# An audio tower kernel: input loaded first, row scales of the first pair spread by TensorE, and new positions for the steps of all stages

## The chip, the cores and the metric

One core of one Trainium2 chip. The metric is device time in microseconds (us) of one execution, the median of several runs; less is better. Beside it stands one profiled execution, whose trace gives every instruction its start, its duration and what released it.

## The reference

```python
# x: 16 batches x 128 channels x 750 steps, f32
fwd = ewma_scan(xt); bwd = ewma_scan(xt[::-1])[::-1]         # carry = 0.1*x + 0.9*carry
h = einsum('btc,dc->btd', (fwd + bwd) * 0.5, W) + b           # D = 256
hidden = layernorm(h)                                          # no gain, no shift
for l in range(2):                                             # N = 64 states
    delta = softplus(hidden @ Wd[l] + bd[l]); u = hidden @ Wi[l] + bi[l]
    decay = exp(-delta * softplus(A_log[l])); drive = delta * u
    hs = scan over t of (s = decay*s + drive)
    hidden = hs @ Wo[l] + bo[l] + (final @ Ws[l] + bs[l])      # class row
h = h + hidden
xf = layernorm(h)
shared = (silu(xf @ shared_gate.T) * (xf @ shared_up.T)) @ shared_down.T   # 512 wide
scores = sigmoid(xf @ router_w.T); sb = scores + correction_bias
# 16 experts in 4 groups; the 2 best groups by the sum of their 2 best, then the 4 best experts
w = scores of the 4 / their sum
routed = sum over the 4 of (w * silu(xf @ gate[e]) * (xf @ up[e])) @ down[e]  # 64 wide each
out = h + shared + routed                                      # 12,000 tokens x 256
```

## The kernel before

The 16 batches are worked in 8 pairs of 1500 tokens. A pair's tokens are cut into three stretches of 500, and those into 12 tiles of 125 tokens. The work falls into three kinds.

- **The chain** turns a pair's input into tokens with their LayerNorm and their place in the experts' lists. Its steps are `ewma`, `ewma_back` (the two scans, VectorE), `tok` (the token product, TensorE, evacuated to `h` and measured by VectorE), `ln1_stats` (variance by VectorE, the power -0.5 by GpSimd, L716), `pre(layer, s)` (both projections of one layer for one stretch), `ssm_log`, `ssm_decay`, `ssm_scan` (softplus, decay, scan), `split`, `carry` and `class_row` (parts of the next layer's input), `y(s, half)` (output product of the last layer, added to `h` by VectorE at L1147), `residual` (GpSimd adds the class row to `h`, L725), `ln2_stats`, `ln2_norm`, `x2t` (transposes), `logit`, the `route_*` and `place_*` steps (top experts and each token's place), `entries` (L1311, the positions), `list` 0 to 11 (GpSimd scatters a tile's entries into the lists in DRAM, L732), and `table` (L1379 to L1382, the first row of each list, needed by the next pair).
- **Shared slots** (S): 12 in a pair, one for each quarter of the shared network's hidden units and stretch of 500 tokens (L1605, L1392).
- **Expert blocks** (B): 99 in all, each 128 entries of one of six lists (one for each pair of groups). GpSimd gathers the rows (L753), TensorE transposes them (`bx`, L1650), multiplies by the weights of two groups (L1630) and transposes the hidden units back (`bh`, L1658), ACT and VectorE scale and split them (L1401, L1406, L1416, L1422), TensorE multiplies by the down weights (L1689), and GpSimd adds the rows to the output in DRAM (`add_to_out`, L764). A B slot of pair q works on entries that earlier pairs put into the lists.

Time is counted in ticks, 24 for each pair. `SHARED` and `ROUTED` (L17, L18) say which ticks hold which kind of slot. The table `CHAIN` (L21) says for each step where it stands on each engine, in ticks from the beginning of the pair's own slots (negative: while the pair before has the slots); `EARLY` (L121) holds exceptions for single pairs, and `PREPARE` (L134) the positions of the weights' preparation. From these `ticks` builds one fixed order of instructions for each engine. Nothing is reordered at run time: an instruction that waits holds up all that stand behind it on its engine. The tables fix only the order; how long a tick lasts comes out of the work.

On TensorE all chain products and the transposes `bx` and `bh` share two PSUM banks, `ch_ps`, used in turn. `bank_is_free` makes each user wait until the user two turns before has been evacuated:

```python
if g is not None and slot(g - 2)[0] == "B":
    in_turn.append(("bh", 0, slot(g - 2)[1]))
if g is not None and slot(g + 2)[0] == "B":
    in_turn.append(("bx", 0, slot(g + 2)[1]))
```

In the first pair nothing is there yet to fill TensorE. SP issues the token weight `tok_w` (L565), then the input of both batches (L567); ACT issues the token bias as the first of its queue. VectorE and TensorE together prepare the token weight (`tokw` 0, L960 and L962 on VectorE), and VectorE then scans. The row scales `rstd` (one number for each token, tokens in the partitions) are needed along the free axis for `pre(0, s)`. Their way is: transpose on TensorE (L1526), ACT to `rstd_rows` (L821), SP stores them to DRAM (L626), and SP loads them back three times, spread to all partitions (L635), into `rb[s]`; VectorE multiplies by them at L1104.

## Time and profile before

| | before |
|---|---|
| three runs, us | 1368.88, 1370.2, 1370.58 (median 1370.2) |
| profiled execution, us | 1365.87 |
| its span (first to last instruction), us | 1364.1 |
| granted TensorE clock, mean | 0.928 of full |
| TensorE busy | 1181.2 us, 87% |
| VectorE busy | 923.1 us, 68% |
| GpSimd busy | 582.2 us, 43% |
| ACT busy | 542.1 us, 40% |
| DMA | 71.04 MB, mean 52 GB/s |

A granted clock of 1.00 is TensorE at 2.4 GHz, 0.50 at 1.2 GHz; a stretch between them spent a part at each. In rows of the trace PE is TensorE, DVE VectorE, POOL GpSimd, SPq and ACTq the sequencers of SP and ACT when they issue DMAs. A row of a timeline gives start, duration, engine, line and operation, and in brackets how long the engine had stood idle before it and what released it.

### The profile page before, as it was taken

How to read it: one execution, taken by the hardware profiler on the slowest of the kernel's cores; microseconds unless marked ns; L12 is line 12 of the kernel's file. 1: busy time of each engine (PE TensorE's matmuls, PEld its weight loads, DVE VectorE, ACT ScalarE, POOL GpSimd, SP SyncE). 2: the span in 40 equal slices, each digit the busy share in tenths (PEclk: the TensorE clock that was granted, in tenths of full speed). 3: DMA queues.
4: the chain of work that ended last, by engine and by line, in shares of the span. 5: the costliest groups of instructions: out<-in, count | busy, mean ns of one | idle time of the engine just before them, and what ended most of it. 6: DMA issues, size and time to landing. Idle time of an engine off the chain costs nothing.

```text
span 1364.1 us, 24631 instructions
## 1 busy us (share of the span) xinstructions
PE 1181.2 (87%) x7454; PEld 1067.0 (78%) x7454; DVE 923.1 (68%) x2326; ACT 542.1 (40%) x893; POOL 582.2 (43%) x428
## 2 busy tenths in 40 slices
PE   3459858987999699987999699987999889998997
PEld 3348647777988688876888689876988788898997
DVE  6786996977578765876578764877578644654443
ACT  1424613542355235532355134442355233223332
POOL 2053272084515643284514634176423632375543
PEclk9558987998999899998999799998999989999999
DMA  3503112121411123121411223121221213223321
GB/s 73 121 27 96 31 29 81 32 52 28 115 32 41 38 55 75 32 49 48 88 41 33 41 55 82 32 46 49 47 74 37 42 47 58 42 51 57 56 34 17
DMA packets 84543, 71.04 MB, mean 52 GB/s; under 512 B 36302, under 2 KB 79119, under 8 KB 84424
## 3 DMA queue, kind: packets, MB, share of 16 engines
q0 software_dynamic: 22272, 25.51, 11.7%
q1 hardware_dynamic: 59920, 43.55, 11.2%
q8 instruction: 72, 1.18, 0.4%
q10 hardware_dynamic: 2232, 0.42, 0.2%
q14 instruction: 47, 0.39, 0.1%
HBM read 32.13 MB, written 38.60 MB: 52 GB/s over the span
## 4 chain that ended last, share of the span: by engine, by line
PE 56%; DVE 15%; issue 11%; POOL 10%; ACT 3%; DMA 3%; SPq 1%; POOLq 0%; DVEq 0%; ACTq 0%
PE gu_ps L1630 15%; PE gu_ps L1605 12%; PE d_ps L1689 10%; PE d_ps L1671 5%; POOL lists L732 4%; PE ch_ps L1582 3%; PE ch_ps L1658 2%; PE ch_ps L1521 2%; POOL block_rows L753 2%; POOL h L725 2%; PE ch_ps L1531 1%; POOL out_dram L764 1%; DMA x_in<-in_x_dram 1%; DVE fw L1049 1%; PE ch_ps L1650 1%
## 5 line engine op out<-in xcount | busy, mean ns | idle before, releaser
L889 ACT ACTIVATE hid<-gu_ps 128x512 f32<-128x512 f32 (+1 forms) x195 | 115.1, 593 | 366.3 <-PE gu_ps L1630 262.1
L764 POOL DMA_INDIRECT out_dram<-block_rows,entry x99 | 157.4, 1590 | 226.2 <-ACT block_rows L901 203.2
L1630 PE MATMUL gu_ps<-gu_hi,bx_hi 128*128 x792 | 243.5, 307 | 10.0 <-issue 10.0
L1630 PE MATMUL gu_ps<-gu_hi,bx_lo 128*128 x792 | 229.5, 290 | 0.0
L1630 PE MATMUL gu_ps<-gu_lo,bx_hi 128*128 x792 | 229.2, 289 | 0.0
L732 POOL DMA_INDIRECT lists<-listed,pos x96 | 126.6, 1319 | 185.5 <-DVE pos L1311 160.0
L1671 PE MATMUL d_ps<-down,hid 128*125 128x256 f32 x768 | 188.1, 390 | 0.0
L1630 PEld LDWEIGHTS gu_ps<-gu_hi,bx_hi 128*128 128x128 f32 x792 | 157.1, 198 | 18.3 <-issue 16.9
L1671 PEld LDWEIGHTS d_ps<-down,hid 128*125 128x125 f32 x768 | 142.9, 194 | 20.0 <-issue 0.3
L1630 PEld LDWEIGHTS gu_ps<-gu_hi,bx_lo 128*128 128x128 f32 x792 | 157.3, 199 | 1.2
L1630 PEld LDWEIGHTS gu_ps<-gu_lo,bx_hi 128*128 128x128 f32 x792 | 155.7, 197 | 0.0
L753 POOL DMA_INDIRECT block_rows<-token_rows,entry x99 | 116.5, 1177 | 49.2 <-issue 25.0
L1422 DVE TENSOR_TENSOR hid_lo<-ch_ps,hid_hi 128x512 fp32r<-128x512 f32 x99 | 67.9, 686 | 97.0 <-ACT hid_hi L906 97.0
L1689 PE MATMUL d_ps<-dr_hi,hid_hi 128*128 x396 | 117.9, 298 | 7.8 <-DVE h L1412 7.8
L1689 PE MATMUL d_ps<-dr_hi,hid_lo 128*128 x396 | 112.4, 284 | 0.0
L1689 PE MATMUL d_ps<-dr_lo,hid_hi 128*128 x396 | 112.3, 284 | 0.0
L720 POOL TENSOR_TENSOR rstd<-mv,mhalf 125x4 f32<-125x4 f32 x24 | 27.8, 1157 | 197.4 <-DVE mv L1090 197.3
L1401 DVE TENSOR_TENSOR gu_ps<-gu_ps,entry 128x512 f32<-128x512 f32 x99 | 69.7, 704 | 26.6 <-PE gu_ps L1630 22.6
L1157 DVE TENSOR_TENSOR x_lo<-ch_ps,x_hi 128x500 fp32r<-128x500 f32 x48 | 32.0, 677 | 80.0 <-ACT x_hi L873 80.0
L901 ACT ACTIVATE block_rows<-d_ps 128x256 f32<-128x256 f32 x99 | 38.0, 383 | 121.1 <-PE d_ps L1689 121.1
L1689 PEld LDWEIGHTS d_ps<-dr_hi,hid_hi 128*128 128x128 f32 x396 | 75.7, 191 | 12.3 <-issue 11.5
L725 POOL TENSOR_TENSOR h<-h,rows 125x512 f32<-125x512 f32 x48 | 65.2, 1378 | 43.3 <-DVE rows L1139 42.9
(271 smaller groups left out, 2981.4 us busy)
## 6 DMA issues: line engine op xcount, KB each, us to landing
token_rows<-xn SPq DMA_DIRECT2D x24, 500.0 KB
out_dram<-h SPq DMA_DIRECT2D x24, 500.0 KB
t<-rstd_scratch SPq DMA_DIRECT2D x24, 250.0 KB, 5.1
x_in<-in_x_dram SPq DMA_DIRECT2D x15, 375.0 KB, 3.5
entry<-lists SPq DMA_DIRECT2D x99, 8.0 KB, 3.0
block_rows<-token_rows,entry POOLq DMA_INDIRECT x99, 2.9
out_dram<-block_rows,entry POOLq DMA_INDIRECT x99, 3.8
lists<-listed,pos POOLq DMA_INDIRECT x96, 2.6
```

Of the source, the lines that this page charges most:

```text
L725: inc(pool.tensor_tensor(hv, hv, row, ALU.add), "res_done")
L732: pool.indirect_dma_start(out=lists, out_offset=bass.IndirectOffsetOnAxis(pos[:, arg:arg + 1], 0), in_=listed[:, arg, :], in_offset=None). ...
L753: pool.indirect_dma_start(out=block_rows[u], out_offset=None, in_=token_rows[0:there, :], in_offset=bass.IndirectOffsetOnAxis(entry[n % UE ...
L764: pool.indirect_dma_start(out=out_rows[0:there, :], out_offset=bass.IndirectOffsetOnAxis(entry[n % UE][:, ID:ID + 1].bitcast(U32), 0), in_ ...
L889: inc(act.activation(hid[g % 4][:, 0:n], gu_ps[:, 2 * (g % 2), 0:n], ACT.Silu), "silu_done")
L1401: inc(dve.tensor_tensor(up, up, w, ALU.mult), "up_weighed")
L1422: inc(dve.tensor_tensor(hid_lo[g % 2][:], ch("bh", 0, n), hid_hi[g % 2][:].bitcast(F32), ALU.subtract), "b_lo")
L1582: last = pe.matmul(bank[0:TP, j * 64:j * 64 + e1], xx[:, k, j * TP:(j + 1) * TP], rw[:, k, 0:e1], start=(n == 0), stop=(n == len(parts) - ...
L1605: last = pe.matmul(bank, w[:, k, ms], xx[:, k, :], start=(k == 0 and q == 0), stop=(k == KD - 1 and q == 2))
L1630: last = pe.matmul(gu_ps[:, 2 * (g % 2) + half, q * GH:(q + 1) * GH], a[n % 2][:, k, :], w[:, k, bass.ds(of, 1), half * GH:(half + 1) * GH ...
L1671: last = pe.matmul(d_ps[0:TP, j, :], hid[g % 4][:, tc], down[:, m, :], start=(m == 0 and j % 2 == 0), stop=(m == M - 1), skip_group_check= ...
L1689: last = pe.matmul(d_ps[:, 2 * (n % 2), :], a[g % 2][:, m * P:(m + 1) * P], rows_[:, bass.ds(of, 1), half * D:(half + 1) * D].rearrange("p ...
```

## The change

- The input is loaded first. `tok_w` goes to ACT's queue, ahead of the bias, which has a signal of its own (`w_tokb`). `tokw` 0 moves from -34.6 to -32.2, that is behind the first batch's forward scan on VectorE.
- The first pair's row scales are spread by TensorE: for each stretch of 500 a new step `rstd_row` multiplies the column of scales, broadcast to 128 columns, by the identity, four times 125 columns, and ACT copies the bank to `rb[s]`. The store and the three loads of the first pair go away; the other pairs keep them.
- With the spread gone from SP for the first pair, SP's `loads` (weights of the shared network and the experts) directly follow the load of the third batch (L617).
- The preload of the exponential's table on ACT goes away for the first pair's second layer (L839).
- `SHARED` and `ROUTED`: the slots at ticks 12 and 13 to 16 change places, so that the B slot of tick 12 is now at tick 16. Many positions in `CHAIN`, `EARLY` and `PREPARE` are new. What they change in the order of each engine, where the work is that the trace shows waiting: on VectorE `entries` come ahead of one evacuation of the second layer (L1114) and two products of a B slot (L1406), and behind one of an S slot (L1392); `table` 1 and `table` 3 come earlier; `y(0,0)` comes behind a product of a B slot; a pair of additions (L1412) comes ahead of `y(0,1)`, where it had stood ahead of `y(1,1)`; and `ln2_norm` 0 (L1093) comes ahead of `y(1,1)`. On GpSimd `list` 9 comes behind the next batch's forward and backward sum (L709), `list` 11 ahead of `residual` 3, and in the first pair ten lists stand ahead of the residual, not nine. On ACT `score_exp` comes half a tick earlier.

```diff
-SHARED = (0, 1, 2, 3, 7, 8, 9, 10, 13, 14, 15, 16)
-ROUTED = (4, 5, 6, 11, 12, 17, 18, 19, 20, 21, 22, 23)
+SHARED = (0, 1, 2, 3, 7, 8, 9, 10, 12, 13, 14, 15)
+ROUTED = (4, 5, 6, 11, 16, 17, 18, 19, 20, 21, 22, 23)
...
-    ("ewma", 0, dict(SP=-32.0, DVE=-33.5, POOL=-29.0, ACT=-28.5)),
+    ("ewma", 0, dict(SP=-33.5, DVE=-33.5, POOL=-29.0, ACT=-28.5)),
-    ("ewma", 1, dict(SP=-23.5, DVE=-28.5, POOL=-27.0, ACT=-26.5)),
+    ("ewma", 1, dict(SP=-25.5, DVE=-28.5, POOL=-27.0, ACT=-26.5)),
-    ("spread", 0, dict(SP=-22.0)),
+    ("spread", 0, dict(SP=-23.5)),
+    ("rstd_row", 0, dict(PE=-22.0, ACT=-21.5)),
+    ("rstd_row", 1, dict(PE=-22.0, ACT=-21.5)),
+    ("rstd_row", 2, dict(PE=-22.0, ACT=-21.5)),
-    ("ssm_log", 1, dict(ACT=-10.0, DVE=-11.0)),
+    ("ssm_log", 1, dict(ACT=-10.0, DVE=-10.5)),
-    ("y", (0, 0), dict(PE=-5.5, DVE=-6.0)),
+    ("y", (0, 0), dict(PE=-5.5, DVE=-5.5)),
-    ("ln2_stats", 0, dict(DVE=-4.5, POOL=-4.5)),
+    ("ln2_stats", 0, dict(DVE=-4.5, POOL=-4.0)),
-    ("ln2_norm", 0, dict(DVE=-3.5, ACT=-3.5)),
+    ("ln2_norm", 0, dict(DVE=-4.0, ACT=-3.5)),
-    ("ln2_stats", 1, dict(DVE=-3.0, POOL=-4.0)),
+    ("ln2_stats", 1, dict(DVE=-2.5, POOL=-2.0)),
-    ("score_exp", 0, dict(ACT=5.5)),
-    ("route_pairs", 0, dict(DVE=7.5)),
+    ("route_pairs", 0, dict(DVE=6.0)),
+    ("score_exp", 0, dict(ACT=5.0)),
-    ("list", 9, dict(POOL=18.5)),
+    ("list", 9, dict(POOL=19.5)),
-    ("table", 1, dict(DVE=16.5)),
+    ("table", 1, dict(DVE=16.0)),
-    ("table", 3, dict(DVE=17.5)),
-    ("list", 11, dict(POOL=20.0)),
+    ("table", 3, dict(DVE=17.0)),
+    ("list", 11, dict(POOL=19.5)),
...
 PREPARE = (
-    (-34.6, "tokw", 0),
+    (-32.2, "tokw", 0),
-    (-21.5, "loads", 0),
+    (-22.0, "loads", 0),
-    (-14.9, "fold", 3),
+    (-16.9, "fold", 3),
-    (3.4, "routed", 1),
+    (2.9, "routed", 1),
...
 # SP
-            sp.dma_start(wraw, tok_w.rearrange("(k p) c -> p k c", p=P)).then_inc(S["w_tok"], 16)
...
 # ACT
-            act.dma_start(tokb_bc[:], tok_b.partition_broadcast(TP)).then_inc(S["w_tok"], 16)
+            act.dma_start(wraw, tok_w.rearrange("(k p) c -> p k c", p=P)).then_inc(S["w_tok"], 16)
+            act.dma_start(tokb_bc[:], tok_b.partition_broadcast(TP)).then_inc(S["w_tokb"], 16)
...
+                elif step == "rstd_row":
+                    wait(act, "ew_lo_done", 2)
+                    wait(act, "rstd_row_mm", arg + 1)
+                    inc(act.activation(rb[arg], ch(step, arg, pair)[:, 0:TT], ACT.Copy), "rb_ev")
...
                 elif step == "ssm_log":
-                    act.preload_act_table(ACT.Exp)
+                    if pair or arg == 0:
+                        act.preload_act_table(ACT.Exp)
...
 # VectorE, pre(0, s)
-                        wait(dve, f"rb{s}", 16 * (pair + 1))
+                        if pair == 0:
+                            wait(dve, "rb_ev", s + 1)
+                        else:
+                            wait(dve, f"rb{s}", 16 * pair)
...
 # TensorE
+                elif step == "rstd_row":
+                    wait(pe, "rstd1", 1)
+                    for j in range(SUB):
+                        last = pe.matmul(bank[:, j * TP:(j + 1) * TP],
+                                         rstd[0][:, arg * SUB + j:arg * SUB + j + 1].broadcast_to([TP, P]),
+                                         ident[0:TP, 0:TP], start=True, stop=True)
+                    inc(last, "rstd_row_mm")
```

## Rows read from the trace of the kernel before

**Rows 1.** The chain that ended last, shares of the span by engine, from the page.

```profile
PE 56%; DVE 15%; issue 11%; POOL 10%; ACT 3%; DMA 3%; SPq 1%; POOLq 0%; DVEq 0%; ACTq 0%
```

**Rows 2.** Windows: stretch, length, busy us of each engine, granted clock, DMA share, GB/s.

```profile
0.00:107.00 107.00, 51.16 (x208) 43.24 (x209) 82.32 (x197) 33.29 (x43) 25.44 (x27) 0.67 0.32 76
...
550.00:700.00 150.00, 133.16 (x843) 120.18 (x842) 103.44 (x257) 61.45 (x102) 67.25 (x49) 0.94 0.23 51
...
1225.00:1364.10 139.10, 126.72 (x1055) 126.09 (x1053) 57.35 (x98) 46.53 (x100) 67.50 (x51) 0.97 0.27 41
```

**Rows 3.** TensorE's waits, 107 to 1200 us: total us, times, longest.

```profile
PE ch_ps L1573 <- DVE hid_lo L1422: 24.1, 4, 6.2
PE ch_ps L1573 <- DVE h L1147: 23.2, 7, 6.6
```

**Rows 4.** Timeline of VectorE in the fourth pair's slots, 607 to 625 us.

```profile
607.01 0.69 DVE L1147 TENSOR_TENSOR h<-ch_ps,h 125x512 f32<-125x512 f32 x1 [5.47 <-POOL h L725]
612.02 1.93 DVE L1082 TENSOR_TENSOR mv<-stats 125x4 f32<-125x4 f32 x1
...
617.43 1.94 DVE L1043 TENSOR_SCALAR ends<-x_in 128x2 f32<-128x2 f32 x1 [1.38 <-DMA x_in<-in_x_dram]
...
624.42 1.28 DVE L1412 TENSOR_TENSOR h<-d_ps,h 125x512 f32<-125x512 f32 x2
```

**Rows 5.** Timeline of GpSimd in the same slots, 598 to 620 us.

```profile
597.99 1.61 POOL L764 DMA_INDIRECT out_dram<-block_rows,entry  x1 [0.30 <-issue]
605.63 3.73 POOL L725 TENSOR_TENSOR h<-h,rows 125x512 f32<-125x512 f32 x3
610.89 1.21 POOL L732 DMA_INDIRECT lists<-listed,pos  x1 [0.30 <-issue]
619.27 1.05 POOL L720 TENSOR_TENSOR rstd<-mv,mhalf 125x4 f32<-125x4 f32 x1
```

**Rows 6.** The first transfer of input: its issue and landing; then its kind's median, from the page.

```profile
L567 SPq DMA_DIRECT2D x_in<-in_x_dram x1: 457/457/457, 1.3 to 1.3; - x1
DMA to landing us min/median/max: 7.1/7.1/7.1
x_in<-in_x_dram SPq DMA_DIRECT2D x15, 375.0 KB, 3.5
```

**Rows 7.** Timelines of the start: VectorE, ACT, TensorE.

```profile
8.15 0.42 DVE L962 SCALAR_TENSOR_TENSOR tw_lo<-gu_ps,tw_hi 128x256 fp32r<-128x256 f32 x1
25.95 0.20 ACT L802 ACTIVATE spt<-vecs 128x2 f32<-128x2 f32 x1 [5.83 <-DMA corr_bc<-ffn_correction_bias_dram]
32.42 0.37 PE L1526 MATMUL ch_ps<-ident,rstd 125*12 125x125 f32 x1 [6.28 <-POOL rstd L716]
32.55 0.76 PE L1543 MATMUL ch_ps<-ew_hi,f_hi 128*128 128x500 f32 x1
38.07 0.73 DVE L1104 SCALAR_TENSOR_TENSOR zt<-ch_ps,cb,t 64x500 f32<-64x500 f32 x1 [8.19 <-DMA t<-rstd_scratch]
41.06 1.06 PE L1484 MATMUL gu_ps<-ident,h 128*128 128x128 f32 x4
66.31 0.94 DVE L1118 TENSOR_TENSOR t<-t 128x750 f32<-128x750 f32 x1 [0.95 <-ACT t L851]
89.62 0.67 DVE L1147 TENSOR_TENSOR h<-ch_ps,h 125x512 f32<-125x512 f32 x1
90.99 0.15 DVE L1093 SCALAR_TENSOR_TENSOR nmr<-mv,rstd 125x4 f32<-125x4 f32 x1
```

**Rows 8.** Timeline of VectorE in the first pair's slots, at 185 us.

```profile
184.75 4.36 DVE L1382 TENSOR_SCALAR table<-route_t 1x6 int32<-1x6 f32 x1
```

**Rows 9.** Timeline of VectorE ahead of the fourth pair's positions.

```profile
574.93 0.60 DVE L1114 TENSOR_SCALAR t<-zt,bias1s 128x750 f32<-128x750 f32 x1
575.45 0.68 DVE L1406 TENSOR_TENSOR hid<-hid,gu_ps 128x512 f32<-128x512 f32 x1
```

**Rows 10.** TensorE's only wait of note in the tail, 1225 to 1364 us.

```profile
PE ch_ps L1650 <- DMA block_rows<-token_rows,entry: 3.5, 1, 3.5
```

More of the change, by code:

```diff
@@ L57 @@
     ("split", (1, 1), dict(ACT=-6.0, DVE=-7.0)),
-    ("residual", 5, dict(POOL=-2.0)),
-    ("y", (0, 0), dict(PE=-5.5, DVE=-6.0)),
+    ("residual", 5, dict(POOL=-1.5)),
+    ("y", (0, 0), dict(PE=-5.5, DVE=-5.5)),
     ("y", (0, 1), dict(PE=-5.0, DVE=-4.5)),
-    ("ln2_stats", 0, dict(DVE=-4.5, POOL=-4.5)),
+    ("ln2_stats", 0, dict(DVE=-4.5, POOL=-4.0)),
     ("y", (1, 0), dict(PE=-4.5, DVE=-4.5)),
-    ("ln2_norm", 0, dict(DVE=-3.5, ACT=-3.5)),
+    ("ln2_norm", 0, dict(DVE=-4.0, ACT=-3.5)),
     ("y", (1, 1), dict(PE=-4.0, DVE=-4.0)),
@@ L101 @@
     ("place_sum", 0, dict(DVE=10.0)),
+    ("route_marks", 2, dict(DVE=12.5)),
     ("list", 1, dict(POOL=13.0)),
     ("list", 2, dict(POOL=14.0)),
-    ("list", 3, dict(POOL=14.0)),
+    ("list", 3, dict(POOL=14.5)),
     ("list", 4, dict(POOL=15.5)),
@@ L123 @@
     (1, "table", 3): dict(DVE=19.5),
-    (1, "list", 11): dict(POOL=22.0),
+    (1, "list", 11): dict(POOL=21.5),
     (1, "list", 6): dict(POOL=16.5),
@@ L129 @@
     (1, "list", 8): dict(POOL=19.5),
-    (1, "table", 0): dict(DVE=14.0),
+    (1, "table", 0): dict(DVE=14.5),
+    (0, "list", 0): dict(POOL=11.0),
+    (0, "ln1_stats", 0): dict(POOL=-22.0),
+    (0, "list", 8): dict(POOL=12.5),
+    (1, "ln2_norm", 1): dict(ACT=-1.5),
+    (1, "x2t", (0, 0)): dict(ACT=-3.5),
+    (1, "x2t", (0, 1)): dict(ACT=-3.5),
+    (0, "residual", 4): dict(POOL=-1.5),
+    (0, "residual", 5): dict(POOL=-1.5),
+    (0, "ln2_stats", 0): dict(POOL=-3.5),
+    (0, "ln2_stats", 1): dict(POOL=-3.0),
+    (0, "ln2_stats", 2): dict(POOL=-1.0),
+    (0, "list", 7): dict(POOL=17.0),
+    (0, "list", 6): dict(POOL=17.0),
+    (0, "list", 9): dict(POOL=17.5),
+    (0, "list", 10): dict(POOL=17.5),
+    (1, "y", (2, 1)): dict(PE=-1.5, DVE=-1.5),
+    (1, "table", 1): dict(DVE=16.0),
+    (1, "table", 2): dict(DVE=17.0),
+    (1, "route_weights", 0): dict(DVE=13.0),
+    (0, "list", 3): dict(POOL=16.0),
+    (0, "list", 4): dict(POOL=17.0),
+    (0, "list", 5): dict(POOL=19.0),
+    (1, "list", 10): dict(POOL=20.5),
+    (0, "ewma_back", 1): dict(DVE=-28.0),
+    (1, "place_hot", 0): dict(DVE=8.5),
+    (0, "list", 11): dict(POOL=19.0),
+    (1, "list", 1): dict(POOL=11.5),
+    (1, "list", 2): dict(POOL=12.5),
+    (1, "list", 3): dict(POOL=13.0),
+    (1, "list", 4): dict(POOL=14.0),
+    (1, "list", 5): dict(POOL=16.0),
+    (1, "rstd_row", 0): dict(ACT=-15.5),
 }
 PREPARE = (
-    (-34.6, "tokw", 0),
+    (-32.2, "tokw", 0),
     (-28.0, "tokw", 1),
@@ L247, in ticks @@
             for step, arg, at in CHAIN:
+                if q and step == "rstd_row" or q == 0 and step in ("rstd_t", "spread"):
+                    continue
                 if engine in at:
@@ L461, in audio_tower_kernel @@
         NAGGR = 7
-        PE_STEPS = ("tok", "rstd_t", "pre", "carry", "class_row", "y", "x2t", "logit", "place")
+        PE_STEPS = ("tok", "rstd_row", "rstd_t", "pre", "carry", "class_row", "y", "x2t", "logit", "place")
         in_turn = []
@@ L486, in bank_is_free @@
             elif was == "rstd_t":
-                wait(pe, "rstd_ev", pair + 1)
+                wait(pe, "rstd_ev", pair)
+            elif was == "rstd_row":
+                wait(pe, "rb_ev", arg + 1)
             elif was == "pre":
@@ L624, in chain @@
                 elif step == "spread":
-                    wait(sp, "rstd_ev", pair + 1)
+                    wait(sp, "rstd_ev", pair)
                     sp.dma_start(rstd_dram[pair].rearrange("t (j p) -> (t j) p", p=TP),
@@ L630, in chain @@
                     wait(sp, "st_lo", 4 * pair)
-                    if pair == 0:
-                        wait(sp, "ew_lo_done", 2)
-                    wait(sp, "rstd_st", 16 * (pair + 1))
+                    wait(sp, "rstd_st", 16 * pair)
                     for s in range(NT):
@@ L714, in chain @@
                     wait(pool, "aggr1", NAGGR * (pair + 1))
-                    wait(pool, "rstd_mm", pair)
+                    if pair == 1:
+                        wait(pool, "rstd_row_mm", NT)
+                    else:
+                        wait(pool, "rstd_mm", pair - 1)
                     inc(pool.tensor_tensor(rstd[0][:], mv[0][:, :, 1], mhalf[:], ALU.pow), "rstd1")
```

46 lines of the change are left out of this document (23 added, 23 removed).

## Prediction

> **What bounds the kernel now.** First the page's chain of work that ended last [rows 1]: more than half is TensorE, then VectorE, then GpSimd. No engine bounds the kernel alone, so a stretch is read by what TensorE waits for. Second, the windows [rows 2]: in the first 107 us TensorE is busy for 51, and the start is bound by VectorE and by waits; in the middle it is busy 133 of 150 us at a granted clock of 0.94; in the tail 127 of 139 at 0.97. A microsecond taken from the middle is worth it only where TensorE stands still for it. Third, TensorE's own waits [rows 3]: two stand out, both at the products of `y` (L1573), both for a bank to be evacuated by VectorE. The one behind `hid_lo` comes four times for 6.0 us each, once in each set of slots of the third to sixth pair; the one behind `h` (L1147) seven times, 23.2 us in all.
>
> Fourth, the timelines of VectorE and GpSimd in one such set [rows 4, 5]. VectorE stood idle for 5.47 us until GpSimd had added the class row to `h`, and began `y(0,0)` at 607.01. GpSimd had begun these additions at 605.63, behind lists, gathers and scatters that follow each other 0.30 apart. VectorE then works without a break to 625, but for 1.38 us for the input, so what stands in that row delays `hid_lo` and TensorE's second stall. So the cause of both stalls is how late GpSimd's row of transfers ends, and this begins when VectorE gives the positions (`entries`). I read the change by that chain.
>
> **The change part by part** (+ is time gained).
>
> *Input first.* The input was issued at 1.3 and took 7.1 us, twice the 3.5 us of later loads [rows 6]. It is issued 0.5 us earlier and with `tok_w` no longer ahead of it; I take a landing near 7.6 in place of 8.4. The forward scan begins that much sooner, but the two operations of `tokw` 0 (L962 has 0.42 us, its partner the same [rows 7]) now stand behind it and not in the wait for the input. 0.8 less 0.84: 0. Bounds: -0.9 if the landing doesn't move, +2.5 if it falls to 3.5 us and the token weight is then what is waited for.
> That both loads of batch 0 and 1 and the weights slow each other is what rows 6 suggest. The Trainium skill (DMA: Bandwidth & Descriptors, Issuing engines are not separate DMA queues) says that DMAs of all issuing engines run on the same 16 engines and interleave, so that another issuer saves issue time alone. By that the term is the 0.5 us of issue less 0.84, that is -0.3; the trace agrees so far.
>
> *The weights' loads.* With the spread gone, SP issues megabytes of them behind the third batch's input, 16 us sooner, beside ACT's twelve small loads, for whose last bytes ACT already waits 5.83 us (L802 at 25.95 [rows 7]). They can be as much slower as the input was at 7.1 against 3.5: -3.6. I take -1.5, as VectorE takes the result up later; the other end is 0.
>
> *Row scales.* Before: TensorE's transpose at 32.42, VectorE goes on at 38.07 after 8.19 us idle [rows 7]. After: three times four products. Four of 128x128 took 1.06 us at half clock (L1484), so the three end at 35.6, and ACT's copies (0.7 each by VectorE's 0.67 for 512 columns) lie beside them but for the last, which `pre(0,0)` doesn't need for its bank. Its three products of 500 columns (first 0.76) take 1.6: 37.2, thus +0.9. Bounds: each copy in series, 32.4 + 3 x 1.76 + 1.6 = 39.3: -1.2; the products at twice the speed and 1.3 less for `pre`: +3.
>
> *Table load dropped.* VectorE waited 0.95 us for ACT in that layer (66.31): +0.95; 0 if the table must come at its use.
>
> *`ln2_norm` 0 ahead of `y(1,1)`.* In the start 90.99 becomes 89.62, and `xn` and its transposes with it: +1.3 (0 to 1.4).
>
> Start: 0 - 1.5 + 0.9 + 0.95 + 1.3 = +1.65 (-5.7 to +7.9).
>
> *First pair's slots.* `table` 3 took 4.36 us beside GpSimd's additions, where a small operation takes 0.15 [rows 7, 8]; ahead of the splits it leaves that stretch: +4.2. One more list (1.21 + 0.30 [rows 5]) stands ahead of the residual: -1.5. +2.7. Bounds 0 and +7, when a second one like it goes too. *Second pair's:* eight lists ahead of the residual before and after: 0 (±1.5).
> The Trainium skill (GPSIMD Engine Reference, Specifications) says that GpSimd's SBUF interfaces are shared with VectorE, and that they contend when VectorE runs in a two-port mode or reads two SBUF inputs. The row's operation has one input of six numbers; by the rule alone it need not be slow there, and the sum would lack the 4.2. The trace shows it slow, and I go by the row.
>
> *Third to sixth pair's slots, four times.* On VectorE `entries` come ahead of L1114 (0.60) and two of L1406 (0.68 each), and behind one S product of the same size (0.67): 1.3 earlier [rows 7, 9]. The B slot that leaves tick 12 takes a scatter (1.61 + 0.30 [rows 5]) out of GpSimd's row ahead of the residual: 1.9. So GpSimd's additions, and `y(0,0)` on VectorE, come 3.2 sooner. From there to `hid_lo` VectorE gets one pair of additions more (1.28), and loses the 1.38 of waiting for the input, whose load is freed sooner, since `list` 9 no longer stands ahead of L709 [rows 4]. 3.2 - 1.3 + 1.4 = +3.3 for each, 13.2 in all; 0 and +5.3 each as bounds (nothing where another wait takes over; with the 2 us of one slow operation more). Cover: `list` 9 now lies behind L709, in time that GpSimd has free; without it, it costs 1.5. *Seventh pair's:* its waits are short: +1.3 (0 to 3.3).
> A new wait comes with the slots: TensorE's `bx` of the moved block now needs the bank of `y(0,0)`, and behind it stand that block's products. As VectorE's row sets the end of both, it moves the wait and adds none, as long as `y(0,0)` is early.
>
> *Earlier `score_exp`, `route_*`, `x2t`, `fold`, `routed`:* at nothing; ACT is idle for most of such a set [rows 2], and VectorE's routing work is the same instructions in another order. If one comes too early it holds its queue by a matmul's wait, 1 us or so; this is in the ranges.
>
> *Tail.* GpSimd's row of lists there is unbroken to TensorE's wait of 3.5 us [rows 10]. It loses a scatter, 1.9, and the positions come 0.6 sooner: +2.5 (0 to 3.5).
>
> **Sum.** 1.65 + 2.7 + 0 + 13.2 + 1.3 + 2.5 = 21.3. The profiled execution took 1365.87 us, 1.8 more than its span; it becomes 1344.6. The median of the runs shown lies 4.3 above the profiled one, so the forecast for a median is 1349.
>
> **The rivals.**
>
> *More (1332).* Two of VectorE's operations in rows 4, of 4 and 2 numbers to a row, took 1.93 and 1.94 us beside GpSimd's additions; elsewhere 0.15. Everything there moves against everything else; if both get free: 2 x 1.8 x 4 = 14, and with shorter stalls the clock (0.94 in the middle, [rows 2]) gives back 3 more. 1349 - 17. Against it: GpSimd's four additions for the input and the residual stay where VectorE has its small operations.
>
> *The middle gives nothing (1363).* The `bx` bank behind `y(0,0)`, or a POOL row that waits for a gather's rows and not for VectorE, takes the 3.3 each: 21.3 - 14.5 = 6.8. For it: GpSimd waits for nothing but issue in rows 5, so what moves ahead of the residual is transfers of other blocks, and the time comes back where these stand now. Against it: VectorE really stood idle for 5.47 us.
>
> *Slower (1378).* `ln2_norm` 0 now stands ahead of `y(1,1)` on VectorE, and waits for GpSimd's power (L720, 619.27 + 1.05 [rows 5]). By the sum VectorE gets there at 621.1 (624.42 less 3.3) and the power ends at about 619.3: 3.2 earlier, and with `list` 11 and half of its neighbours ahead of it. Lateness beyond 1.8 us goes whole into `y(1,1)`, whose bank TensorE wants. From 7 us on it outweighs the gain of the middle and the rest (5 x 5.2 = 26); at 7.6 it makes 29 us: 1378. For it: three lists, a residual and an addition of the input now stand there; against it: they are 1.2 to 1.8 us each [rows 5], and some stood there before.
>
> *No change (1370).* Gains of the middle and the new places of some thirty steps cancel.
>
> **How the numbers follow.** 0.48 for the forecast (its own range 1342 to 1357), 0.15 for more, 0.18 for the middle giving nothing, 0.11 for slower, 0.08 for no change. A range from 1330 to 1370 leaves out the slower case, half of no change and the far end of more: 2 in 10. A measurement of this kernel tells 0.2%, 2.7 us, from nothing. Faster by more than that: 0.48 + 0.15 + 0.18 = 0.81; within it 0.08; slower 0.11.
>
> **What would show it.** In the start: VectorE's L1104 at about 37 (after the earlier parts' shift), the ACT wait in front of L802 longer than 5.8, no table load in layer 1. In the first pair's slots: no L1382 over 1 us. In the middle: VectorE's first L1147 some 3 us sooner after the positions, idle time before it under 3 us, TensorE's waits for `hid_lo` near 3 us in place of 6, and a clock above 0.94. In the tail TensorE's wait near 1 us. It would be wrong if L1573 or L1650 waited as long as before, for another releaser (`y(0,0)`'s evacuation, a power of GpSimd), or if the waits of VectorE for L720 added up.

## The result, and the profile after

| | before | after |
|---|---|---|
| median, us (4 runs each) | 1369.54 (1367.34 to 1370.58) | 1342.15 (1340.87 to 1345.77) |
| profiled execution, us | 1365.87 | 1340.87 |
| its span, us | 1364.1 | 1339.1 |
| granted TensorE clock, mean | 0.928 | 0.936 |

The ratio is 0.9834, 95% interval 0.9805 to 0.9862: 27.4 us faster by the medians, 25.0 by the profiled executions. The forecast was 1349 and 21.3 us. Of the 6.9 us by which the median beats the forecast, 3.7 are the profiled execution (1344.6 was worked out, 1340.87 measured); the rest is the distance between the median and the profiled execution, taken at 4.3 us from the runs before and 1.3 here.

To see where the 25.0 us came from, I cut both spans at one operation that every set of slots has: VectorE's evacuation of `y(2,0)` (L1147, after L1196). All times below are differences between such marks. The stretch of one pair's slots runs from one mark to the next; the tail is what follows the last mark.

| stretch, from mark to mark | before | after | gained | forecast |
|---|---|---|---|---|
| start | 101.75 | 102.00 | -0.25 | +1.65 |
| first pair's slots | 114.63 | 112.03 | +2.6 | +2.7 |
| second | 117.83 | 122.92 | -5.1 | 0 |
| third to sixth, together | 624.35 | 600.81 | +23.5 | +13.2 |
| seventh | 148.48 | 148.00 | +0.5 | +1.3 |
| tail | 257.06 | 253.34 | +3.7 | +2.5 |

The total hides a start that gained nothing and a second set that lost. I take the stretches in turn.

**The start.** VectorE's timeline of the changed kernel:

```profile
4.17 0.17 DVE L1089 TENSOR_SCALAR ends<-x_in 128x2 f32<-128x2 f32 x1 [1.70 <-DMA x_in<-in_x_dram]
...
15.38 0.94 DVE L1106 TENSOR_TENSOR t<-t 128x750 f32<-128x750 f32 x1
16.23 0.68 DVE L1116 TENSOR_TENSOR h<-ch_ps,tokb_bc 125x512 f32<-125x512 f32 x1
...
30.48 0.17 DVE L1067 TENSOR_SCALAR spt<-vecs 128x2 f32<-128x2 f32 x1 [5.30 <-ACT spt L846]
...
39.66 0.73 DVE L1153 SCALAR_TENSOR_TENSOR zt<-ch_ps,cb,t 64x500 f32<-64x500 f32 x1 [7.78 <-PE ch_ps L1600]
```

and ACT's and SP's of the same time:

```profile
20.61 0.54 ACTq L834 DMA_DIRECT2D corr_bc<-ffn_correction_bias_dram  x1
...
23.95 2.33 ACTq L839 DMA_DIRECT2D h<-in_L_ffn_router_w_dram  x1
28.42 0.20 ACT L842 ACTIVATE spt<-vecs 128x2 f32<-128x2 f32 x1 [11.24 <-DMA corr_bc<-ffn_correction_bias_dram]
```

```profile
16.73 0.43 SPq L637 DMA_DIRECT2D hid<-L_ffn_shared_gate_w_dram  x1
17.21 0.71 SPq L637 DMA_DIRECT2D h<-n_L_ffn_shared_up_w_dram  x1
17.96 7.00 SPq L626 DMA_DIRECT2D block_rows<-in_L_ffn_gate_w_dram  x2
```

A gain is made and then lost. The input lands at 4.1 us in place of 8.4, and the token evacuations begin at 16.23, 3.3 us sooner than before (19.51). Then VectorE stands for 5.30 us in front of softplus, where it had no wait before, because ACT is at L842 2.5 us later than it was at L802 [rows 7], though its small loads began 2.9 us sooner. So L1153, which was L1104, comes at 39.66, 1.6 us later than before.

**The middle.** VectorE in the fourth pair's slots, the operations that answer to [rows 4]:

```profile
603.41 0.69 DVE L1196 TENSOR_TENSOR h<-ch_ps,h 125x512 f32<-125x512 f32 x1 [3.21 <-POOL h L764]
...
606.37 1.29 DVE L1461 TENSOR_TENSOR h<-d_ps,h 125x512 f32<-125x512 f32 x2
...
610.02 1.64 DVE L1132 TENSOR_SCALAR mv<-mv 125x4 f32<-125x4 f32 x1
...
613.32 0.21 DVE L1089 TENSOR_SCALAR ends<-x_in 128x2 f32<-128x2 f32 x1
...
619.26 0.17 DVE L1139 SCALAR_TENSOR_TENSOR nmr<-mv,rstd 125x4 f32<-125x4 f32 x1 [0.59 <-POOL rstd L759]
```

`y(0,0)` has 3.21 us of idle time before it in place of 5.47. The first operation on the new input (L1089, L1043 before) takes 0.21 us in place of 1.94 and waits for nothing. TensorE in the same slots:

```profile
604.16 0.44 PE L1707 MATMUL ch_ps<-ident,block_rows 128*128 128x128 f32 x2 [1.40 <-DVE h L1196]
...
612.67 0.44 PE L1707 MATMUL ch_ps<-ident,block_rows 128*128 128x128 f32 x2 [0.66 <-DVE h L1196]
617.80 0.58 PE L1630 MATMUL ch_ps<-wo_hi,states 128*125 128x256 f32 x1 [3.26 <-DVE hid_lo L1471]
```

The two stalls of 3.77 and 6.16 us became 1.40 and 3.26. The first has moved to the transposes of the moved block, which now wait for `y(0,0)`'s bank, as the prediction said. Over 107 to 1200 us TensorE's waits that answer to [rows 3] are (L1630 is the product of `y`, L1573 before; L1707 is `bx`, L1650 before):

```profile
PE ch_ps L1630 <- DVE hid_lo L1471: 12.9, 4, 3.3
PE ch_ps L1707 <- DVE h L1196: 11.6, 9, 3.2
...
PE ch_ps L1630 <- DVE h L1196: 6.7, 3, 3.5
```

Before, `bx` had waited 3.9 us for `h` there as well, so 51.2 us of waiting became 31.2. The granted clock rose too: the window that answers to the second of [rows 2] is

```profile
550.00:700.00 150.00, 139.35 (x893) 125.32 (x892) 108.86 (x284) 68.78 (x112) 70.69 (x49) 0.98 0.24 53
```

with 0.98 in place of 0.94. How much is wait and how much is clock, the windows of the third to sixth set show, before and after, each with the same 3596 matmuls:

```profile
334.21:958.57 624.36, 560.77 (x3596) 507.83 (x3595) 441.23 (x1109) 261.78 (x433) 279.37 (x198) 0.95 0.24 53
...
336.95:937.75 600.80, 554.34 (x3596) 501.35 (x3595) 430.95 (x1108) 266.81 (x437) 284.18 (x198) 0.98 0.25 55
```

TensorE's idle time (length less busy time) fell from 63.6 to 46.5 us, that is by 17.1, and its busy time by 6.4, at a granted clock of 0.98 in place of 0.95. Together they are the 23.5.

**The tail.** TensorE's wait for `block_rows` there is 1.04 us, at 1208.79, in place of 3.5 [rows 10]. That is 2.5 of the 3.7 us.

### The profile page after: what moved, and what is told of

Its sections match the earlier page's. It is cut to its first block, busy times and chain, and to the rows that moved or that the text cites. A ratio compares the mean times of both kernels' runs of the same rounds, so it can differ in the third digit from the quotient of the medians.

```text
span 1339.1 us, 24682 instructions
## 1 busy us (share of the span) xinstructions
PE 1175.4 (88%) x7477; PEld 1059.6 (79%) x7477; DVE 912.5 (68%) x2326; ACT 548.9 (41%) x899; POOL 587.9 (44%) x428
## 4 chain that ended last, share of the span: by engine, by line
PE 52%; DVE 17%; issue 14%; POOL 11%; ACT 3%; DMA 2%; ACTq 0%; POOLq 0%; DVEq 0%; SPq 0%
PE gu_ps L1687 15%; PE gu_ps L1662 11%; PE d_ps L1746 9%; POOL lists L771 6%; PE d_ps L1728 4%; PE ch_ps L1639 3%; PE ch_ps L1715 2%; PE ch_ps L1570 2%; POOL block_rows L792 2%; DVE h L1461 1%; PE ch_ps L1588 1%; POOL h L764 1%; PE ch_ps L1707 1%; DVE h L1196 1%; DVE gu_ps L1450 1%
## 5 line engine op out<-in xcount | busy, mean ns | idle before, releaser
L771 POOL DMA_INDIRECT lists<-listed,pos x96 | 133.3, 1388 | 183.5 <-DVE pos L1360 157.6
L792 POOL DMA_INDIRECT block_rows<-token_rows,entry x99 | 116.9, 1181 | 49.9 <-issue 23.5
L941 ACT ACTIVATE bx_hi<-ch_ps 128x256 fp32r<-128x256 f32 x99 | 37.8, 382 | 122.0 <-PE ch_ps L1707 121.8
L764 POOL TENSOR_TENSOR h<-h,rows 125x512 f32<-125x512 f32 x48 | 66.8, 1408 | 42.0 <-DVE rows L1188 41.6
```

Of the source, the lines that this page charges most:

```text
L764: inc(pool.tensor_tensor(hv, hv, row, ALU.add), "res_done")
L771: pool.indirect_dma_start(out=lists, out_offset=bass.IndirectOffsetOnAxis(pos[:, arg:arg + 1], 0), in_=listed[:, arg, :], in_offset=None). ...
L792: pool.indirect_dma_start(out=block_rows[u], out_offset=None, in_=token_rows[0:there, :], in_offset=bass.IndirectOffsetOnAxis(entry[n % UE ...
```

## The experiments

There were three sessions of four kernels. Each ratio is against runs of the kernel before in the same session. The changed kernel was measured again in two of them, the second and the third, and its own time differs by session (next part). So an experiment of the first session (`x_first`, `loads_wait`, `softplus_behind`, `table3_pair1`) can't be compared with the changed kernel by its ratio. The stretches between marks carry the argument, each from one profile, and the ratios stand beside them.

### The changed kernel measured twice more

> The changed kernel itself, on the chip of the next three. The last four runs and their runs of the kernel before were all on one chip and some us slower than the first; in their profiles TensorE has gaps of 0.2 to 2.5 us in the last 180 us that the trace puts down to nothing but issue, and the changed kernel's first profile has fewer. Theory: that is the chip, and the ratio to the kernel before is again 0.983 to 0.986. Rival: the first ratio was a lucky one and this one is about 0.99.

Measured: 1355.52, ratio 0.9911 (0.9889 to 0.9932).

> The changed kernel again, as the measure for the next three on their chip. The two measurements so far gave 0.983 and 0.991 of the kernel before, on two chips; the profiles agree within 0.3 us up to 648 us and differ by 4.6 in the last pair's slots and by 10 in the tail. Theory: the difference is the chip, in what the trace calls issue; on a third chip it is one or the other. Rival: it varies from run to run.

Measured: 1341.53, ratio 0.9802 (0.9774 to 0.983). This profiled execution, 1350.0 us at a mean granted clock of 0.888, was the slowest of its seven. The stretches of the three profiles of one and the same program:

| | first | second | third |
|---|---|---|---|
| start | 102.00 | 101.70 | 102.61 |
| second pair's slots | 122.92 | 122.97 | 123.68 |
| third to sixth | 600.81 | 605.40 | 608.60 |
| tail | 253.34 | 264.40 | 253.13 |

TensorE's idle time in the third to sixth set is 46.5, 46.4 and 46.2 us: it repeats, and the 7.8 us by which these sets differ are busy time. Between the first two profiles the tail differs most, by 11 us. Sixty us of it, from some 77 us behind its mark on, in the first and in the second profile, windows of equal length:

```profile
1163.00:1223.00 60.00, 58.94 (x436) 55.79 (x435) 31.98 (x74) 17.52 (x38) 42.65 (x37) 1.00 0.30 58
```

```profile
1167.60:1227.60 60.00, 53.71 (x352) 48.66 (x351) 27.87 (x67) 14.16 (x30) 40.28 (x35) 0.95 0.26 54
```

The second has 84 matmuls fewer in the same time. Between its matmuls are gaps such as

```profile
1197.34 0.66 PE L1715 MATMUL ch_ps<-ident,hid 128*128 128x128 f32 x4 [0.77 <-issue]
1198.74 0.39 PE L1687 MATMUL gu_ps<-gu_hi,bx_hi 128*128 x1 [0.74 <-issue]
```

in which TensorE waited for nothing that the trace names. The first profile has one such wait in its tail, of 0.3 us. Over the whole tail TensorE's waits are 1.3 us in the first profile and 7.0 in the second, and its busy time is 243.1 and 248.2 us. The theory "it is the chip" fell: the first session ran on the same chip as the third, and its profiles have the long tail (265.5 to 268.6), the third's have the short one (253.1 to 253.7). In the second session the tails are 259.0 to 265.5. But "by session" is not shown for every kernel: the medians of the kernel before are 1374.57, 1367.66 and 1367.99, alike in the second and third session, where the changed kernel's differ by 14 us. There is one profile of each kernel in a session, and none of the kernel before in these three. What it is stays open. The gain of the change lies between 0.9% and 2.0%, by session.

### The input first, alone

```diff
-            sp.dma_start(wraw, tok_w ...).then_inc(S["w_tok"], 16)        # SP, ahead of the input
...
+            act.dma_start(wraw, tok_w ...).then_inc(S["w_tok"], 16)       # ACT, first
...
-    (-34.6, "tokw", 0),
+    (-32.2, "tokw", 0),
```

> The kernel before with one part of the change: the input is loaded first, the token weight goes to ACT's queue, and its preparation stands behind the first forward scan. In the changed kernel the input landed after 3.4 us in place of 7.1, and VectorE's first token evacuation began at 16.23 in place of 19.51. Theory: that gain of 3.3 us is the order of loads alone, and here it reaches the end, since the weights' loads stay where they were and ACT's twelve small loads are not crowded: VectorE's softplus at about 25.5 in place of 28.48, span 3.3 us shorter (about 1361), ratio about 0.998. Rival: ACT's small loads, issued 3 us sooner, land no sooner than before (their last bytes are what holds VectorE), and then the token evacuations are 3.3 us sooner and the softplus is not: less than 1 us at the end. The prediction's term was 0.

Measured: 1372.53, ratio 0.9985 (0.9965 to 1.0005). Token evacuations at 16.49, softplus at 25.47, the start's mark at 98.81 in place of 101.75: the theory holds, 2.9 us reach the end of the start. The ratio neither shows nor excludes them: by the medians `x_first` is 2.0 us faster, and the interval reaches from 4.8 us faster to 0.7 slower. Its profiled execution (1377.56) is one of the slowest of twelve. In it the first pair's slots took 115.77 us in place of 114.63 and the second pair's 122.72 in place of 117.83. Of these 4.9 us, 2.2 are lost in small steps by 298 us, and 2.7 in the last ten us. From 298 to 327 us the two profiles stand within 0.7 us of each other. Then they part; ten us from about the same matmul on, before and here:

```profile
327.61:337.61 10.00, 10.00 (x88) 10.00 (x87) 5.26 (x12) 2.06 (x5) 3.37 (x3) 1.00 0.06 6
```

```profile
328.05:338.05 10.00, 10.00 (x67) 10.00 (x67) 3.32 (x8) 1.68 (x4) 3.26 (x3) 0.72 0.05 5
```

In both TensorE is busy for all of the 10 us, at 1.00 and at 0.72, with 88 and 67 matmuls. TensorE's longer waits in the 30 us ahead were the same two (5.6 and 1.9 us); `x_first` had one of 1.1 us at 298.79 and one of 0.6 at 320.61 more. Whether these set the clock is not shown.

### The weights' loads held back

```diff
                 if what == "loads":
+                    sp.wait_ge(S["w_in"], 16 * W_IN)
```

> The changed kernel with one wait more: SP issues the weights' loads only when ACT's small loads have landed. In the changed kernel ACT waited 11.24 us for them (L842 at 28.42) and VectorE then 5.30 us for ACT. Theory (the loads crowd each other): with the wait ACT's L842 comes at about 23.0 (2.9 us sooner than the 25.95 of before), VectorE's softplus at about 25.2 and the row scales 5 us sooner; the end 4 to 5 us sooner, span about 1334.5, if the weights, now issued at about 23, still land before they are needed at 41. Rival 1: the small loads are slow by themselves (one column of two numbers for each partition), and the big loads have no part in it: nothing gained. Rival 2: the weights come too late, and their preparation delays the first shared slots: slower by some us.

Measured: 1358.3, ratio 0.9879 (0.9851 to 0.9907), in the session with the long tail. The start took 97.58 us in place of 102.00. ACT's timeline:

```profile
20.71 0.51 ACTq L835 DMA_DIRECT2D corr_bc<-ffn_correction_bias_dram  x1
...
22.92 0.34 ACTq L840 DMA_DIRECT2D h<-in_L_ffn_router_w_dram  x1
23.34 0.20 ACT L843 ACTIVATE spt<-vecs 128x2 f32<-128x2 f32 x1 [5.82 <-DMA corr_bc<-ffn_correction_bias_dram]
```

L843 at 23.34 (23.0 was expected), no wait at VectorE's softplus (25.76), and no engine waited for the weights, issued from 23.33 on. The big loads beside them had also slowed the issuing: the last small load took ACT 2.33 us to issue there, 0.34 here. The rows show as well what the 5.82 is: nearly all of it is ACT's own time for issuing twelve loads (16.70 to 23.26), counted as idle time. In the prediction I took the 5.83 of [rows 7] for a wait for late bytes.

### Softplus behind the statistics

```diff
-    (-23.9, "softplus", 0),
+    (-22.9, "softplus", 0),       # VectorE: behind ln1_stats (-23.0)
```

> The changed kernel with VectorE's three softplus operations behind ln1_stats (seven small operations) in place of ahead of them; nothing else moves. Theory (what costs at 30.48 is only that the row scales' variance stands behind a wait that it has no need of): GpSimd's power begins at about 26 in place of 31.96, TensorE's row products at about 28.6; ACT is held until 30.4 by the same small loads, so the first copy is at 30.4 in place of 36.56, and VectorE's first L1153 at about 34 in place of 39.66: 5 to 6 us at the end, span about 1333.5. Rival: the crowding itself holds other things as well (weights, staging), and less than 2 us is left at the end.

Measured: 1359.1, ratio 0.987 (0.9839 to 0.9902). L1153 at 34.25, the start 96.61 us: 5.4 less, as expected. So the price of the crowding was real (ACT's L842 is still at 27.80), but it had to be paid only because three small operations that need it stood ahead of seven that don't.

### Table 3 of the second pair earlier

```diff
 EARLY = {
-    (1, "table", 3): dict(DVE=19.5),
```

> The changed kernel without the exception that puts table 3 of the second pair at 19.5: it goes to 17.0, ahead of the residual, as in the other pairs. In the changed kernel its six operations stand between y(0,0) and y(0,1) of the third pair at 300.31 to 304.25, two of them at 1.39 and 1.65 us in place of 0.2 beside GpSimd's additions, and this set of slots lost 5 us against the kernel before. Theory: these 3.9 us are taken from the row of operations that sets TensorE's stalls there; 3 to 4 us at the end, span about 1335.5. Rival: the loss of this set is the new wait for the bank of y(0,0) (3.17 and 3.51 us at L1707 and L1630), which stays; under 1 us.

Measured: 1359.0, ratio 0.9884 (0.986 to 0.9908). The second pair's slots took 119.36 us in place of 122.92: 3.6 of the 5.1 lost there. In the changed kernel these rows stood between `y(0,0)` and `y(0,1)`, beside GpSimd's additions (its L764 from 294.83 to 298.6, its L745 from 299.81 on):

```profile
300.31 1.39 DVE L1428 TENSOR_TENSOR route_t<-route_t,step_c 1x72 f32<-1x72 f32 x1
...
302.69 1.65 DVE L1431 TENSOR_SCALAR table<-route_t 1x12 int32<-1x12 f32 x1
304.25 0.67 DVE L1196 TENSOR_TENSOR h<-ch_ps,h 125x512 f32<-125x512 f32 x1
```

The new bank's wait, the rival, explains at most the rest.

### The positions alone

The kernel before with `SHARED`, `ROUTED`, `CHAIN`, `EARLY` and `PREPARE` of the changed one, without `rstd_row` and with `tokw` 0 at -34.6; its loads, waits and preloads are those of before.

> The kernel before with all new positions, and without the input first, without the spreading by TensorE and with both table preloads. Theory: the gain of the change is in the positions (from the end of the first pair's chain at 106 to the end the changed kernel gained 25 us, while its start lost 0.3). The start is then that of before but for the third to eighth step: the weights' loads still follow the spread, so they crowd nothing, and the span is about 1339 to 1341. Rival: parts of the start's change carry the middle (a shifted order, the bank's turn), and less than 20 us is gained here.

Measured: 1357.95, ratio 0.9927 (0.9906 to 0.9947), where the changed kernel had 0.9911. The start took 100.65 us (1.1 less than before, 1.35 less than the changed kernel), the third to sixth set 604.91 (605.40 for the changed kernel in that session). So the gain of the middle is in the positions and slots, and the parts of the start that gave the change its name show no gain as they stand; by the medians the changed kernel is 2.4 us faster than this one, with overlapping intervals. The expected span of 1339 to 1341 was missed: 1355.4. Some 9 us of that are the session's long tail (262.6 in place of 253.3). The rest is the third to sixth set (4.1 more than in the first profile) and the seventh, 151.61 in place of 148.00, less what the start gained.

### The slots back, and the slots alone

```diff
-SHARED = (0, 1, 2, 3, 7, 8, 9, 10, 12, 13, 14, 15)
-ROUTED = (4, 5, 6, 11, 16, 17, 18, 19, 20, 21, 22, 23)
+SHARED = (0, 1, 2, 3, 7, 8, 9, 10, 13, 14, 15, 16)
+ROUTED = (4, 5, 6, 11, 12, 17, 18, 19, 20, 21, 22, 23)
```

in the changed kernel (slots_back), and the reverse in the kernel before (slots_alone).

> The changed kernel with the slots of before (B at tick 12, S at 13 to 16). Theory: the moved slot's scatter (1.91 us of GpSimd ahead of the residual) and the positions after L1114 and two products (1.3 us of VectorE) are what makes y(0,0) 3.2 us earlier in each of five sets of slots; back with them, VectorE waits for the residual for over 5 us as before, and 10 to 16 us of the 25 go: span about 1352. Rival: what gains in the middle is that VectorE no longer waits for the input and does its first small scan operation outside GpSimd's addition (1.38 + 1.73 us), which stays here: 5 us or less lost.

> The kernel before with the moved slots alone. Putting the slots back in the changed kernel lost 4.5 us in each of the third to sixth pair's sets. Theory 1 (the slots by themselves do it: a scatter less ahead of the residual, and the pair of additions L1412 out of the row behind y(1,0)): 4 us or more gained in each of four, span near 1348. Theory 2 (they only work with the positions set for them: table 3, list 9, entries, the power): less than 2 us in each, or a loss; span 1356 or more. The prediction's terms give 1.9 less 1.3 for this part alone: 0.6 for each.

Measured: slots_back 1360.99, ratio 0.9944 (0.9924 to 0.9963); slots_alone 1362.84, ratio 0.9972 (0.9951 to 0.9993). By stretches:

| | before | slots alone | other positions alone (slots_back) | both (first profile) |
|---|---|---|---|---|
| second pair's slots | 117.83 | 123.28 | 119.50 | 122.92 |
| third to sixth | 624.35 | 617.92 | 623.43 | 600.81 |
| tail | 257.06 | 253.08 | 258.98 | 253.34 |

(slots_back ran in a session whose other tails are 262 to 266, so its tail can't be compared.) In length, the new positions without the slots gain 0.9 us in the four sets, the slots without the positions 6.4, both 23.5 (15.8 to 23.5 over the three profiles). The windows show what lies behind it, slots alone and slots back:

```profile
336.07:953.99 617.92, 562.45 (x3596) 508.61 (x3595) 440.44 (x1108) 261.89 (x433) 282.37 (x198) 0.96 0.24 53
```

```profile
333.39:956.82 623.43, 567.01 (x3596) 513.53 (x3595) 435.57 (x1109) 266.97 (x437) 280.13 (x198) 0.95 0.24 53
```

| third to sixth set | before | slots alone | slots back | both, three profiles |
|---|---|---|---|---|
| TensorE idle | 63.6 | 55.5 | 56.4 | 46.5, 46.4, 46.2 |
| TensorE busy | 560.8 | 562.5 | 567.0 | 554.3, 559.0, 562.4 |

In idle time the two halves nearly add up: 8.1 and 7.2 us alone, 17.1 to 17.4 together. What does not add up is the busy time, which is longer than before in both halves. Busy time also moves by 8 us between profiles of one and the same program, and each half has one profile, so how much of this belongs to the halves is open. By the medians slots_back keeps 6.7 us of the 12.1 that the changed kernel gained in its session, and slots_alone 5.2 of 26.5 in the third session. The slots alone also lose 5.5 us in the second set, and their tail has TensorE's wait for `block_rows` down to 0.6 us.

Where the slots are back, VectorE's rows in the fourth pair's slots read

```profile
604.84 0.69 DVE L1196 TENSOR_TENSOR h<-ch_ps,h 125x512 f32<-125x512 f32 x1 [5.67 <-POOL h L764]
...
613.86 0.47 DVE L1089 TENSOR_SCALAR ends<-x_in 128x2 f32<-128x2 f32 x1 [1.51 <-DMA x_in<-in_x_dram]
...
621.29 1.76 DVE L1139 SCALAR_TENSOR_TENSOR nmr<-mv,rstd 125x4 f32<-125x4 f32 x1 [0.63 <-POOL rstd L759]
```

The wait for the residual and that for the input are back, and `nmr` ahead of `y(1,1)` meets GpSimd's addition. With the slots alone VectorE waits 2.59 us for the residual at 604.05 and 0.16 for the input, but a small operation took 1.79 (L1086) and another 0.89 (L1043).

### List 9 back

```diff
-    ("list", 9, dict(POOL=19.5)),
+    ("list", 9, dict(POOL=18.5)),
```

> The changed kernel with list 9 ahead of the forward and backward sum (L745) again, in the second to seventh pair's slots. In the kernel before VectorE waited 1.38 us for the input there and its first operation on it took 1.94 us beside GpSimd's addition; in the changed one neither is there. Theory: the sum starts 1.5 us later, the input's load is freed 1.5 us later (it would land at about 613.8, VectorE arrives at 613.3) and its wait is 0.5 us or so, while the slow operation comes back in some sets: 0.5 to 2 us in each of five, span 1342 to 1349. Rival: nothing there was on the path, and the time is the same (1339) or less, since lists 10 and 11 don't move.

Measured: 1360.96, ratio 0.9939 (0.9913 to 0.9965); third to sixth set 603.50 us, where the changed kernel of that session has 605.40. In these sets nothing is lost in the profile, as the rival said; but this profiled execution (1353.54) is the fastest of seven, and the median is 5.4 us above the changed kernel's in its session (1355.52), with intervals that overlap. So a loss of some us is neither shown nor excluded. The wait for the input does come back, 0.94 us, but the slow operation ahead of it is gone:

```profile
612.25 0.17 DVE L1089 TENSOR_SCALAR ends<-x_in 128x2 f32<-128x2 f32 x1 [0.94 <-DMA x_in<-in_x_dram]
```

### The mends together

> The changed kernel with three mends together: SP's weight loads wait for ACT's small loads, VectorE's softplus operations stand behind ln1_stats, and table 3 of the second pair goes ahead of the residual. Alone they made the end of the first set of slots 4.2 and 5.2 us, and the end of the second 3.2 us sooner. The first two work on the same wait: with both, ACT is through the small loads at 23 to 25 and VectorE's row is not held at all, so the row scales come when the token evacuations end: power at 26, first L1153 at about 33, 6.5 us sooner than the changed kernel. With the table 9 to 10 us in all against after_third, ratio to the kernel before lower by 0.007. Rival: gains of the start are lost in a later wait (the weights' arrival at 23 plus 7 us for each of the large ones), and it is 6 us or less.

> The same with the slots of before in the second pair alone. With the slots of before in all pairs the second set ended 3.4 us sooner, while the four after it lost 18 us. Theory: the moved slot costs in the set in which its bank's wait for y(0,0) has no earlier residual to show for it: 3 us less than three_mends. Rival: it was table 3's slow operations met by another order, which are gone in three_mends: no difference, or worse.

Measured in the third session, beside the changed kernel's 1341.53: three_mends 1333.15, ratio to the kernel before 0.9749 (0.9721 to 0.9777); three_and_slots1 1331.63, ratio 0.9725 (0.9695 to 0.9756). The start took 97.21 and 96.52 us, the second set 117.25 and 116.12. So three_mends beats the changed kernel by 8.4 us by the medians (9 to 10 were expected), and the kernel before by 2.5%. The mends of the start don't add up: 4.4 and 5.4 alone, 5.4 together (6.5 were expected). The slots of before in the second pair give 1.1 us more there in the profile, less than the 3 expected; the two ratios' intervals overlap, so which of the two is better is unclear.

## Why the prediction was right, and where it was not

**What bounds the kernel** held. TensorE's two stalls in each of the middle sets were the thing to look at: its idle time there fell by 17.1 of the 23.5 us. Their cause was how late GpSimd's row of transfers ends, and VectorE's row behind it. The other 6.4 are busy time, at a higher granted clock, which the sum had at nothing and only the rival "more" had, at 3.

**Input first**, 0 in the sum: +3.3 at the token evacuations, outside its bound of +2.5. The step that failed took the landing at 7.6, with the input still slowed by the other load. The trace shows 3.4 us from issue to landing with `tok_w` in another queue:

```profile
DMA to landing us min/median/max: 3.4/3.4/3.4
```

The rule of the Trainium skill (DMA: Bandwidth & Descriptors, Issuing engines are not separate DMA queues), by which the term would be -0.3, did not hold here as I had used it: the input landed in half the time. Two things changed at once, the order of the loads and the queue of `tok_w`, and no run here separates them.

**The weights' loads**, -1.5 (bounds -3.6 and 0): from the first token evacuation to softplus 14.25 us in place of 8.97, that is -5.3. That crowding costs was right; the size was wrong and its bound too. The bound was taken from the slowing of one large load, where twelve small ones with their issuing were slowed, and the 5.83 us of [rows 7] were no wait for bytes. loads_wait and softplus_behind show it.

**Row scales and table load**, 0.9 + 0.95: from softplus to `y(0,0)` 48.27 us in place of 49.56, +1.3 together. x_first, without both, has 49.64. From the row scales' first matmul to L1153 it is 5.25 us in place of 5.65, +0.4: the three groups of products took 4.3 us and not 3.2. The other +0.9 lies behind L1153, as worked out for the table load. **`ln2_norm` 0**, +1.3: from `y(0,0)` to `y(2,0)` 23.25 in place of 23.71, +0.5. The step was on the path (TensorE's wait for `xn`) only in part. Start: 3.3 - 5.3 + 1.3 + 0.5 = -0.25.

**First pair's slots**, +2.7: measured +2.6. The number agrees, its parts do not: this was luck. Up to `y(0,0)` the gain is 4.5 (85.92 us in place of 90.47), since two operations of `table` 3 were slow before, of 4.36 [rows 8] and 2.73 us, and are 0.55 and 0.16 now; VectorE then waits 2.46 us for the residual, which comes one list later. From `y(0,0)` to the mark 1.9 are lost (26.11 in place of 24.17), which the sum had at nothing.

**Second pair's slots**, 0 with ±1.5: -5.1. This step failed. "Eight lists before and after" looked only at GpSimd's row; VectorE's row between `y(0,0)` and `y(0,1)` got the pair of additions (1.28) and slow table operations more, 8.04 us in place of 4.19. table3_pair1 gives 3.6 of it back. The rest is not settled: slots_alone loses 5.5 there, slots_back 1.7, and x_first, which moves none of these steps, 4.9.

**Third to sixth**, 4 x 3.3: measured 5.9 each. From the last mark to `y(0,0)` of the fourth pair's slots the gain is 2.8 where 3.2 was worked out (116.25 and 113.47 us). The moved scatter was worked out at 1.9, and slots_alone gains 2.2 there; the positions at 1.3, and slots_back gains 0.6. From there to TensorE's release behind `hid_lo` it is 2.2 (16.63 and 14.39), where +0.1 was worked out. The term that was missing is the operation on the input, 1.94 down to 0.21: the half of the rival "more" that came true. The rest, some 0.9 in this set, lies behind that release: 0.5 of idle time put to issue, and 0.4 of busy time at a granted clock of 0.85 in place of 0.83. The term for the wait of 1.38 was wrong in what it gains. `list` 9 behind the sum does free the input's load 1.5 us sooner: from the residual to the sum it is 4.97 us, and 6.47 with list 9 back. But with list 9 back VectorE reaches the input's first operation as soon after `y(0,0)` as without (9.94 and 9.91 us), because the operation of 1.64 us ahead of it (L1132) is gone. The pair of additions L1412 and this wait are one thing; VectorE does the additions in the time in which it had waited.

**Seventh pair's**, +1.3: +0.5. `y(0,0)` came 2.9 us sooner (111.21 in place of 114.14), and 2.5 were lost behind it, where the row to `y(0,1)` took 6.10 us in place of 3.51.

**The slower rival** had its mechanism right: VectorE waits 0.59 us for GpSimd's power at 619.26, so the slack that I put at 1.8 is none. It did not decide, since it needed 7. **The middle gives nothing** was wrong as to the bank: the wait moved to L1707 and shrank.

**Tail**, +2.5: +3.7. TensorE's wait for `block_rows` fell by 2.5, as worked out; with the slots alone it is 0.6, so it goes with the scatter that left. The other 1.2 us are mostly busy time (244.04 and 243.07), and tails of one and the same program differ by more.

Of the signs named ahead, two were missed: L1153 came at 39.66 and not at 37, and the idle time in front of `y(0,0)` is 3.21 us, not under 3.

The total was nearer than its terms, and that is luck: errors of -1.9 and -5.1 in the start and the second set stand against +10.3 in the middle.

## What to carry to other kernels

When an engine works through a fixed row, ask of each wait in it which of the operations behind it need what is waited for: three operations of 0.2 us held back the start by 5 us. Move large loads forward only past small ones that nobody waits for; a load that nobody needs for 20 us is best issued behind the small ones. And judge new positions by the idle time of the engine that bounds the stretch before going by its length: the idle time repeated to 0.3 us over three profiles of one program, where the length moved by 8, and by it the two halves of this change gave 8.1 and 7.2 us alone and 17 together.

## What the runs showed of the hardware that was not expected

- VectorE's smallest operations, of one to twelve numbers in a row, mostly took 0.15 to 0.2 us. In the fourteen profiles 141 of them took 1.0 to 4.4 us, and every one of these ended within 0.11 us of the end of a `TENSOR_TENSOR` of GpSimd. The 4.36 us of L1382 began at 184.75, while GpSimd issued a scatter, and ended at 189.11, with the last of the three additions that followed (189.07). So the price is not a fixed slowing but the time until GpSimd is through.
- The Trainium skill (GPSIMD Engine Reference, Specifications) limits the contention to VectorE's two-port modes and operations with two SBUF inputs. The prediction took one input to mean that the rule doesn't apply; but the slow operations with one input (L1382 4.36, L1043 1.94, L1132 2.62, L1431 1.65, and 61 more) are all `TENSOR_SCALAR`, and nothing here says that they don't run in a two-port mode. The rows do not contradict the rule.
- Two profiles that stand within 0.7 us of each other for 30 us can part by 3 us in the next ten: 10.00 us of busy TensorE at a granted clock of 1.00 and at 0.72 in the second pair's slots.
- In the third session's profile of the changed kernel the clock is given as 0.95 in the tail (1100 to 1300 us), which has one gap of 0.4 us, and yet the tail took 253.13 us, as at 0.99 (253.34). What that figure means there is open.
- Gaps of TensorE put to issue add up to 4.7 to 9.4 us in every tail of the first and second session, and to 0.2 to 0.7 us in those of the third, whatever the kernel; the tails with them are 6 to 15 us longer. The first and third session ran on one chip.
